# Attention stage: a ring of three probability buffers instead of four, and the end-of-group copies and divisions in another order

## The reference

```python
q1, k1, q2, k2, v = (heads(x @ w.T) for w in (q1_w, k1_w, q2_w, k2_w, v_w))
attn1 = softmax(q1 @ k1.T / sqrt(128)); attn2 = softmax(q2 @ k2.T / sqrt(128))
out = (attn1 - lam * attn2) @ v
x = layernorm(x + out @ o_w.T)
q, in_scale = per_token_quant_int8(x)
x = layernorm(x + fp16((q @ weight.T) * in_scale * w_scale + bias))
```

## Time and profile before

| | us |
|---|---|
| median of 3 runs (3202.0 to 3204.85) | 3204.62 |
| the profiled execution, device time | 3200.92 |
| its span, slowest core (core 1) | 3199.4 |
| spans of the 8 cores | 3192.5 to 3199.4 |
| PE busy | 2947.9 (92%) |
| DVE busy | 1270.1 (40%) |
| ACT busy | 1300.0 (41%) |
| mean granted clock of TensorE | 0.984 |

### The profile page before, as it was taken

The page is one execution under the profiler, slowest core; times in us unless marked ns, Lnnn a source line. Parts: engine busy times, 40 slices in busy tenths (PEclk is TensorE's granted clock), DMA queues, the critical chain, the costliest instruction groups (busy, mean ns, idle before and its releaser), DMA issues.

```text
span 3199.4 us, 45007 instructions; the slowest of 8 cores (3192.5 to 3199.4 us)
## 1 busy us (share of the span) xinstructions
PE 2947.9 (92%) x16640; PEld 1446.8 (45%) x16640; DVE 1270.1 (40%) x1569; ACT 1300.0 (41%) x1363; POOL 44.8 (1%) x85
## 2 busy tenths in 40 slices
PE   0999999999999999999999999999999999886997
PEld 0544454545454545454545454545454544433443
DVE  0133434343333333333333333343434246666676
ACT  0171717171717171707070707070707073444222
POOL 0000000000000000000000000000000000000000
PEclk9999999999999999999999999999999999998998
DMA  9666010101011111111111111010100042446233
GB/s 157 147 182 173 10 24 17 24 17 23 18 20 21 21 21 20 21 19 22 17 25 17 24 16 25 13 28 13 28 1 7 16 137 76 114 124 203 89 111 119
DMA packets 93426, 172.77 MB, mean 54 GB/s; under 512 B 68160, under 2 KB 68160, under 8 KB 86688
## 3 DMA queue, kind: packets, MB, share of 16 engines
q0 software_dynamic: 14016, 86.38, 14.2%
q1 hardware_dynamic: 79200, 83.51, 8.3%
HBM read 174.07 MB, written 50.33 MB: 70 GB/s over the span
## 4 chain that ended last, share of the span: by engine, by line
PE 86%; DVE 6%; another core or an unknown queue 2%; issue 2%; ACT 1%; DMA 1%; DVEq 0%; SPq 0%; ACTq 0%
PE psB L236 14%; PE psA L236 14%; PE pO L272 7%; PE psA L253 7%; PE pO L273 7%; PE pS L274 7%; PE pS L275 7%; PE psB L253 6%; PE psA L224 4%; PE psB L224 4%; PE pffnA L718 3%; PE pffnB L718 3%; DVE sc_ L43 2%; PE pattnL L504 1%
## 5 line engine op out<-in xcount | busy, mean ns | idle before, releaser
L311 ACT ACTIVATE pb<-psA 128x1024 bf16<-128x1024 f32 x512 | 524.1, 1024 | 1268.2 <-PE psA L253 1268.2
L311 ACT ACTIVATE pb<-psB 128x1024 bf16<-128x1024 f32 x512 | 526.4, 1028 | 123.8 <-PE psB L253 123.8
L236 PE MATMUL psB<-xTb,wq 128*128 128x512 bf16 x2048 | 462.9, 379 | 0.0
L236 PE MATMUL psA<-xTb,wq 128*128 128x512 bf16 x2048 | 462.9, 379 | 0.0
L43 DVE RECIPROCAL r<-sc_ 128x512 f32<-128x512 f32 x128 | 429.2, 3353 | 13.9 <-DVE r L43 0.5
L272 PE MATMUL pO<-pb,vv 128*128 128x512 bf16 x960 | 365.7, 381 | 74.5 <-DVE sc_ L43 50.6
L43 DVE COPY sc_<-pS 128x512 f32<-128x512 f32 x128 | 88.6, 692 | 791.1 <-PE pS L280 784.5
L273 PE MATMUL pO<-pb,v 128*128 128x512 bf16 x960 | 365.8, 381 | 0.0
L274 PE MATMUL pS<-pb,ones 128*128 128x512 bf16 x960 | 365.4, 381 | 0.0
L275 PE MATMUL pS<-pb,ones 128*128 128x512 bf16 x960 | 365.3, 381 | 0.0
L253 PE MATMUL psB<-q,k 128*128 128x512 bf16 x1024 | 304.5, 379 | 21.5 <-DVE k L43 10.9
(11 more groups left out here) (97 smaller groups left out, 2166.7 us busy)
## 6 DMA issues: line engine op xcount, KB each, us to landing
wq<-wqkv POOLq DMA_DIRECT2D x15, 2560.0 KB, 20.0
xin<-x SPq DMA_DIRECT2D x16, 1024.0 KB, 8.7
out<-oo SPq DMA_DIRECT2D x16, 1024.0 KB, 4.7
xTb<-xT POOLq DMA_DIRECT2D x4, 2048.0 KB, 40.7
stg<-wo POOLq DMA_DIRECT2D x16, 512.0 KB, 6.4
wob<-stg SPq DMA_DIRECT2D x16, 512.0 KB, 2.7
stg<-wffn POOLq DMA_DIRECT2D x16, 512.0 KB, 4.3
wfb<-stg SPq DMA_DIRECT2D x16, 512.0 KB, 2.7
```

The source lines that it names most:

```text
L236: mm = te.matmul(projb[g % 2][:, 0:512], wslice(m + 1, c), xT_sb[:, c * S + qt * 512: c * S + qt * 512 + 512], start=(c == 0), stop=(c == ...
L311: sc.activation(pb_sb[:, (s % 4) * 1024:(s % 4) * 1024 + 1024], sbank[c % 2][:], AF.Exp, scale=INV_SQRT_HD,).then_inc(sEXP, 1)
```

## The change

It has three parts. The ring pb goes from four slots to three, and PE issues the four matmuls of chunk k-2 behind the scores of chunk k, where it was chunk k-3. ACT does the two copies of a group directly behind that group's sixteenth exponential, where it was behind the third exponential of the next group. DVE does `divide(grp-2)` behind the sum copies of group grp, where it was ahead of them. The number of instructions of each kind stays the same.

```diff
-            pb_sb = Eb(nc.sbuf_tensor("pb", [128, 4096], BF16))
+            pb_sb = Eb(nc.sbuf_tensor("pb", [128, 3072], BF16))
...
-                        b = (s % 4) * 1024
+                        b = (s % 3) * 1024
...
                     for k in range(QT * NC_):
                         s_issue(k)
-                        if k >= 3:
-                            pv_issue(k - 3)
-                    pv_issue(QT * NC_ - 3)
+                        if k >= 2:
+                            pv_issue(k - 2)
                     pv_issue(QT * NC_ - 2)
                     pv_issue(QT * NC_ - 1)
...
             def _(sc):
-                def ocopy(grp):
+                for grp in range(H * QT):
+                    for c in range(NC_):
+                        s = grp * NC_ + c
+                        sc.wait_ge(sS, sS_after[(grp, c)])
+                        if s >= 3:
+                            sc.wait_ge(sPVD, s - 2)
+                        sc.activation(
+                            pb_sb[:, (s % 3) * 1024:(s % 3) * 1024 + 1024],
+                            sbank[c % 2][:], AF.Exp,
+                            scale=INV_SQRT_HD,
+                        ).then_inc(sEXP, 1)
                     sc.wait_ge(sPO0, grp + 1)
                     if grp >= 3:
                         sc.wait_ge(sCB, grp - 2)
...
-                    if c == 2 and grp >= 1:
-                        ocopy(grp - 1)
-                ocopy(H * QT - 1)
...
                     for qt in range(QT):
                         grp = h * QT + qt
-                        if grp >= 2:
-                            divide(grp - 2)
                         ve.wait_ge(sPS0, grp + 1)
...
                         ve.tensor_copy(sc_sb[:, b + 512:b + 1024], pS1[:], inc=(sOC, 1, grp + 1))
+                        if grp >= 2:
+                            divide(grp - 2)
```

## The result

The changed kernel takes 3369.86 us (median of 9 runs), the kernel before 3204.42 (median of 10): ratio 1.0516, 95% interval 1.0505 to 1.0528. The forecast was 3369. In the profiled executions the slowest core's span is 3368.3, core 6, against 3199.4.

The account below looks back on a forecast made before the run. PE, busy 92% of the span, was taken to bound the kernel. Terms 25.9 - 35.4 - 9.0 + 139.5 + 34.5 + 10.4 = +165.9 on the profiled 3200.9 gave 3366.8, taken as 3369 us; range 3330 to 3395.

Parts of the forecast that it names:

- The sum: Whole kernel: all terms together +165.9 us on the profiled 3200.9, giving 3366.8, taken as 3369.
- The head border: Border between heads, 15 times: the division ahead of DVE's V casts adds 9.30 us to PE's wait, +139.5 us.
- The clock term: V tiles behind the head-border wait: slow clock of 2.3 us each, bounds 0 and 2.34, 15 times, +34.5 us.
- Rival 1: Borders between heads: clock does not fall or is back at once, the 34.5 goes, 3335 us; chance 0.09.
- The group border: Between groups inside a head, 48 times: PE loses 1.82 us waiting on ACT, against 1.28 on DVE, +25.9 us.
- The head start: Start of a head's groups: 2.30 us gained at 15, 0.85 at the first, -35.4 us; clock there -9.0 us.
- Behind attention: Stage after attention: DVE has three divisions left instead of two, shift between 9.3 and 11.5, +10.4 us.
- Rival 2: Group borders: longer idle lowers the clock, 1.8 us at each of 48, 3455 us; chance 0.05.
- Rival 3: Head borders: no wait comes because DVE divides under PE's work, faster at 3186 us; chance 0.03.
- Rival 4: Ring of three stalls ACT, so the change does not act as written; no size, chance in the remainder (others 0.03).

Follow-up runs that it names:

- The filler run: Changed kernel plus 40 unused 128x512 matmuls between the second and third V tile of 15 heads; 3340.45 us, ratio 1.0425.
- the run with the distance alone: Kernel before with ring of three and distance two; ACT's copies stay behind the third exponential, DVE's order as before; 3313.26 us, ratio 1.0326.
- The row of waits: Changed kernel with none, one reciprocal, both reciprocals or all of the division at the head border: 3186.62, 3273.33 to 3275.45, 3330.85, 3369.86 us.
- the ring of four: Changed kernel with DVE's order of before and ring pb at four slots again; 3188.73 and 3190.16 us, against 3186.62 with three.

## Why the prediction was right

**The sum** was met term by term, but the last microsecond is luck: the V tiles cost 171.5 us (15 x 11.43) where 174.0 was counted, and the groups gave back less than the 18.5 counted (16.6: the first head, which the table leaves out, took 1.4 us more in its groups, 89.83 to 91.27). The two misses nearly cancel.

**The head border** was the term that decided, and it was read from one row of slack: DVE's first cast came 0.2 us too late for PE even before. That the division's 9.30 us would be added whole is shown by the trace (9.35 printed) and by DVE's part alone at 3388.70, where 3389 was expected. That nothing later in the head gives it back is shown by the unchanged groups (89.40 with and without DVE's part).

**The clock term** of 2.3 us a border measured 11.43 - 9.3 = 2.1; 15 times that is 32 where I had 34.5. It was taken from two rows far from the place, and it held on the mean. As an upper bound the 2.34 did not hold: at the border shown the four slow tiles take 6.35 us where four tiles at 0.90 take 3.6. The filler run shows that it is the clock and not DVE catching up. Rival 1 is out: by its sum it would have been 3335. The Trainium skill ("TensorE: Matmul & The Clock Gate", section "What's actually happening") has the throttled clock as the default, which activity releases. The traces agree: where the 40 unused matmuls fill the wait, no V tile behind it is slow. The same page's figure of 81 ns between matmuls of 128 columns (section "Back-to-back issue gap") does not hold here; the V tiles take 0.89 us for 16, 56 ns each.

**The group border**: 1.82 counted, 1.81 read; 1.28 before. **The head start**: 2.30 gained, and the slow stretches there gone but for the first head. Together these give -1.20 a head where the sum had -1.16, and a kernel 17.0 us faster without DVE's part, where 18.5 was counted.

**Behind attention**: +10.5 for +10.4, which is partly luck. The slow stretch there was larger than the upper bound I gave it (9.65 - 6.91 = 2.74, not 2.21), and so on all eight cores. Directly behind it every core is 12.05 us later than before, counted from the start of this stage; at the end only 10.5 remain on the mean. What gave back the other 1.5 was not followed up.

**Rival 2** did not happen in this change: over heads 2 to 16 of all eight cores no clock was lost in the groups. But the run with the distance alone shows that it was closer than my chance of 5% says: the printed wait was 1.65, and at 2.29 the clock falls at over a third of the borders, at 2.57 every time. The 1 in 20 rested on an argument about two gaps close together against one; that argument is wrong, since one longer gap is enough.

**Rival 3** would have needed DVE to finish under PE's two tiles. The row of waits (0, 3.45, 6.9, 9.3) shows that even the shortest piece of the division goes in whole.

**Rival 4**, a ring of three that stalls ACT, is out by the ring of four, which was not faster.

## What to carry to other kernels

Before moving work on an engine that looks idle (DVE 40% busy), look for the place in the loop where the engine that bounds the kernel has the least cover against it, here two small tiles at the border between heads, and count what would stand in that queue; the same work is free at three of four places and costs 11.4 us at the fourth. Price a wait of the bounding engine twice, once for its length and once for the slow clock that may follow it: here nothing behind 1.65 us printed, and 1.7 to 2.1 us on the mean behind 3.5 and more. Where several buffers are freed one after another, let each consumer wait for its own; that gave 36 us here, by a wait ahead of each of the four matmuls in place of a common one.

## What was not expected of the hardware

A wait of 3.5 us at the V tiles was followed by a slow stretch at 118 of 120 borders, but not always at once: at the border shown the first tile behind it took 0.89 us and the next ones 1.45 and 1.7. At group borders a printed wait of 1.65 us in otherwise unbroken work did not lower the clock, and one of 2.29 us did so at 132 of 360, with the same matmuls around it each time. Why at some and not at others, no run here shows. Here is the stretch from 240 to 2620 us (the third number from the end is the clock) of the kernel without DVE's part, which has the waits of 1.65, and then of the kernel with the distance alone, which has those of 2.29:

```profile
240.00:2620.00 2380.00, 2293.41 (x13404) 1143.53 (x13403) 857.35 (x915) 1028.64 (x1075) 19.63 (x37) 1.00 0.13 28
```

```profile
240.00:2620.00 2380.00, 2224.73 (x12730) 1108.09 (x12913) 810.87 (x879) 970.50 (x1010) 11.95 (x23) 0.98 0.12 24
```

No run here has a single wait in the groups whose printed length lies between 1.65 and 2.29 us, so what such a wait costs stays open.
